# States of two directions summed on TensorE ahead of one product with C, and depthwise convolutions in 32-column tiles with their vertical taps on partitions

## The reference

```python
dA = jnp.exp(dt[:, :, None] * A)
h = dA * h + (dt * u_t)[:, :, None] * B_t[:, None, :]
y = jnp.einsum('bdn,bn->bd', h, C_t) + Dv * u_t
```

## Time and profile before

| | us |
|---|---|
| median of 3 executions | 24551.71 |
| lowest, highest | 24547.85, 24555.85 |
| span of the profiled execution, first to last instruction | 24540.0 |

### The profile page before, as it was taken

The page is one execution under the profiler, slowest core; times in us unless marked ns, Lnnn a source line. Parts: engine busy times, 40 slices in busy tenths (PEclk is TensorE's granted clock), DMA queues, the critical chain, the costliest instruction groups (busy, mean ns, idle before and its releaser), DMA issues. The chain is left out here.

```text
span 24540.0 us, 382078 instructions
## 1 busy us (share of the span) xinstructions
PE 20189.7 (82%) x128858; PEld 8709.5 (35%) x128858; DVE 22873.0 (93%) x21013; ACT 12682.8 (52%) x17667; POOL 8605.8 (35%) x4999
## 2 busy tenths in 40 slices
PE   5888888888888888888888888888888888888886
PEld 2333333333333333333333333333333333333332
DVE  5999999999999999999999999999999999999997
ACT  2555555555555555555555555555555555555554
POOL 2333333333333333333333333333333333333332
PEclk8888888888888888888888888888888888888886
DMA  2222222222222222222222222222222222222222
GB/s 72 75 77 66 78 76 68 78 71 72 77 66 78 76 67 78 72 71 78 68 76 76 67 78 75 68 78 69 74 79 66 78 74 69 78 70 73 77 67 64
DMA packets 646853, 1792.27 MB, mean 73 GB/s; under 512 B 76999, under 2 KB 87059, under 8 KB 644760
## 3 DMA queue, kind: packets, MB, share of 16 engines
q1 hardware_dynamic: 624280, 1726.94, 24.6%
q10 hardware_dynamic: 20480, 38.29, 0.5%
HBM read 1707.39 MB, written 44.96 MB: 71 GB/s over the span
## 5 line engine op out<-in xcount | busy, mean ns | idle before, releaser
L1502 POOL TENSOR_TENSOR drive<-du,Bb 128x784 f32<-128x784 f32 x3072 | 5678.1, 1848 | 14964.6 <-DVE drive L1135 14964.6
L461 PE MATMUL scan_sum<-prod,fold 64*64 64x392 f32 x40960 | 6186.6, 576 | 2824.0 <-DVE prod L1135 2821.4
L461 PE MATMUL bank<-pad,dg 64*64 64x392 f32 x61312 | 7421.5, 512 | 159.5 <-ACT pad L862 133.2
L862 ACT ACTIVATE decay_even<-delta,alog 128x784 f32<-128x784 f32 x3072 | 2818.1, 917 | 8475.7 <-DVE state L1292 8429.1
L1135 DVE TENSOR_TENSOR prod<-state,Cb 128x784 f32<-128x784 f32 x6144 | 6228.4, 1014 | 0.0
L1292 DVE TENSOR_TENSOR_SCAN state<-decay,drive 128x784 f32<-128x784 f32 x3072 | 5831.4, 1898 | 234.0 <-POOL drive L1502 16.0
L1292 DVE TENSOR_TENSOR_SCAN state<-decay_even,drive 128x784 f32<-128x784 f32 x3072 | 5500.0, 1790 | 336.9 <-ACT decay_even L862 172.1
L461 PEld LDWEIGHTS bank<-pad,dg 64*64 64x64 f32 x61312 | 3279.4, 142 | 3858.5 <-issue 3191.3
L461 PEld LDWEIGHTS scan_sum<-prod,fold 64*64 64x64 f32 x40960 | 1647.1, 146 | 6313.9 <-issue 4578.5
L1135 DVE TENSOR_TENSOR drive<-du,Bb 128x784 f32<-128x784 f32 x3072 | 2966.8, 966 | 55.1 <-issue 55.1
L862 ACT ACTIVATE decay<-delta,alog 128x784 f32<-128x784 f32 x3072 | 2862.7, 934 | 1.6
(11 more groups left out here) (179 smaller groups left out, 16842.7 us busy)
## 6 DMA issues: line engine op xcount, KB each, us to landing
Bb<-bc_rows SPq DMA_DIRECT2D x2048, 392.0 KB, 3.7
Cb<-bc_rows SPq DMA_DIRECT2D x2048, 392.0 KB, 4.2
xin<-in_x SPq DMA_DIRECT2D x64, 294.0 KB, 4.2
x_kept<-xin ACTq DMA_DIRECT2D x64, 294.0 KB, 4.4
x<-x_kept SPq DMA_DIRECT2D x64, 294.0 KB, 3.0
out_dram<-t SPq DMA_DIRECT2D x64, 294.0 KB, 2.6
crossed<-pwm ACTq DMA_DIRECT2D x128, 96.0 KB, 2.2
delta<-in_x SPq DMA_DIRECT2D x8, 1176.0 KB, 7.5
```

Source lines behind the costliest of these rows:

```text
L461: return pe.matmul(out, lhsT, rhs, start=start, stop=stop)
L862: return act.activation(out, in_, f, bias=bias, scale=scale, **more)
L1502: pool.tensor_tensor(drive[:, j % 2, :], du[:, m, :], Bb[:, q % SLOTS, :], ALU.mult).then_inc(drive_r.sem, 1)
```

## The change

The units are laid out anew: each has 64 channels on partitions 0 to 63 in one direction and the same channels on 64 to 127 in the other direction that runs the same way along L. Units come in 48 pairs, two states of the same channels and directions. There are still 96 scans, 96 decays and 96 drives. After a pair's second scan TensorE adds the two directions of both states with `fold` into a PSUM tile `S` (two states times 64 channels on partitions): four matmuls of 128x64 tiles. VectorE then does one product with C for the pair, read from `S`, and TensorE adds the two states into `Y` with two matmuls. The product of pair p-1 stands behind the first scan of pair p. Rings: `prod` 2 deep instead of 6, odd decays 2 instead of 3 and each asked for straight behind the even one, `state` 3. `S` takes two PSUM banks, so `Y` and `P` have one bank each; every use of `P` is a numbered round, filled by TensorE (`bank_filled`) and read by ScalarE or VectorE (`bank_read`), and each side waits for the other. B has a row per state for each third of the channels: 48 loads a sample; C has 24 pairs of half loads.

For the convolutions, the 576 channels go through `P` in nine chunks of 64; ScalarE's SiLU puts each chunk's padded image in SBUF, SP stores it to DRAM (2 DMAs a chunk) and loads it again five times, shifted by one row each, so that 24 channels times 5 vertical taps lie on 120 partitions (`rep`): 12 sets of 5 DMAs. One convolution tile is then 5 horizontal taps times 4 matmuls of 120x32, each with 32 output columns; there are 12 such tiles. The 3x3 one is alike: 3 stores of 2 DMAs, 3 sets of 6 loads, 36 matmuls of 96x32. Its result is copied to the other 64 partitions by DMA from ScalarE's queue (6 a sample). GpSimd fills the taps by 12 tensor_tensor instructions of 120x320 a sample in place of the diagonals. The expert stacks, `pww` and `dww`, no longer stay in SBUF and are loaded for each sample. A table gives the steps of the lead their slots: the 21 expansions and convolution tiles stand in 21 of the first 23 pairs, and ScalarE reads each one pair later; the tail is spread over units 15 to 94.5. The core of the diff:

```diff
-T0 = 5
-M0 = 9
+T0 = 6
+G = 4
+GC = C // G
+KT = 5
+KP = KT * GC
+TAPS = T0 * KT * G
+M0 = HID // 64
...
-KS = (0, 1, 3, 4, 2, 5)
-DECAYS = 3
-PRODS = 6
+DECAYS = 2
+PRODS = 2
+STATES = 3
+BSLOTS = 4
 SLOTS = 2
-UNITS = [(g, n, k) for g, ks in ((0, (0, 1, 3, 4)), (1, (2, 5))) for n in range(NS) for k in ks]
-NU = len(UNITS)
+PAIRS = [(s, m, r) for s in range(S3) for m in range(NS // 2) for r in range(2)]
+NP = len(PAIRS)
+NU = 2 * NP
+TURNS = NP // 2
+GROUP = NP // S3
...
-        Y = ps("scan_sum", 1024)
+        Y = ps("scan_sum", 512)
+        S = ps("state_sum", 1024)
         DP = ps("decay_even", 1024)
         TT = ps("pair", 1024)
-        PP = ps("bank", 1024)
+        P = ps("bank", 512)
         T = [TT[:, 0:512], TT[:, 512:1024]]
-        P = [PP[:, 0:512], PP[:, 512:1024]]
...
+            def shifted(i, span, h):
+                for t in range(T0):
+                    first, last = C * t // 64, (C * t + C - 1) // 64
+                    yield max(AT["expand", last] + READ + 2.0, AT["conv", t - 1, h] + 2.0 if t else 0.0)
+                    if t >= 1:
+                        sp.wait_ge(bank_filled.sem, bank(span, "conv", t - 1, h))
+                        alone()
+                    for c in range(first, last + 1):
+                        stored, count = image_out(c)
+                        sp.wait_ge(stored.sem, stored.at(i, count))
+                        alone()
+                    if t == 0 and not later(i):
+                        sp.wait_ge(s_border.sem, 16 * 2 * IMAGES)
+                    loaded, _ = rows_in(t, h)
+                    for dy in range(KT):
+                        src = hid_dram[C * t:C * t + C, PW * (14 * h + dy):PW * (14 * h + dy) + HROWS].rearrange("(g c) l -> c g l", g=G)
+                        sp.dma_start(rep[GC * dy:GC * dy + GC, h, :, :], src).then_inc(loaded.sem, 16)
...
+            def conv(i, span, t, h):
+                for dx, wait in enumerate((0.0, 0.3, 0.6, 1.2, 1.5)):
+                    yield AT["conv", t, h] + wait
+                    if dx == 0:
+                        pe.wait_ge(bank_read.sem, bank(span, "conv", t, h) - 1)
+                        loaded, count = rows_in(t, h)
+                        pe.wait_ge(loaded.sem, loaded.at(i, count))
+                        pe.wait_ge(taps_r.sem, taps_r.at(i, 2 * t + 2))
+                    for g in range(G):
+                        src = rep[0:KP, h, g, :].rearrange("p (y x) -> p y x", x=PW)[:, :, dx:dx + HW]
+                        last = mm(P[32 * g:32 * g + 32, 0:HALF], taps[:, t % 2, G * dx + g, :], src, start=dx == 0, stop=dx == KT - 1)
+                last.then_inc(bank_filled.sem, 1)
...
             def scan(i, *between):
-                for j, (g, n, k) in enumerate(UNITS):
-                    if j >= 1:
-                        summation(i, j - 1)
-                    go_on(between, j + 1)
+                for p in range(NP):
+                    if p >= 1:
+                        summation(i, p - 1)
+                    elif later(i):
+                        summation(i - 1, NP - 1)
+                    go_on(between, 2 * p + 1)
+                    pe.wait_ge(state_r.sem, state_r.at(i, 2 * p + 2))
+                    if p >= 1 or later(i):
+                        pe.wait_ge(prod_r.sem, prod_r.at(i, p))
+                    for h in range(2):
+                        for e in range(2):
+                            j = 2 * p + e
+                            last = mm(S[64 * e:64 * e + 64, 512 * h:512 * h + HALF], fold[:, :], half(state[:, j % STATES, :], h))
+                    last.then_inc(folded.sem, 1)
+                    go_on(between, 2 * p + 2)
                 go_on(between, END)
-                summation(i, NU - 1)
...
+            def summation(i, p):
+
+                s, m, r = PAIRS[p]
+                if p % GROUP == 0:
+                    if s >= 1 or later(i):
+                        pe.wait_ge(y_r.sem, y_r.at(i, s))
+                    pe.wait_ge(xc_in.sem, xc_in.at(i))
                     for h in range(2):
-                        last = mm(Y[64 * h:64 * h + 64, bank:bank + HALF], weights[rows], term[rows, h * HALF:(h + 1) * HALF],
-                                  start=start, stop=stop)
-                return last
-
-            def summation(i, j):
-
-                g, n, k = UNITS[j]
-                if n == 0 and k == (0, 2)[g]:
-                    skipped(i, g)
-                pe.wait_ge(prod_r.sem, prod_r.at(i, j + 1))
-                if g == 0:
-                    alone()
-                term = prod[:, j % PRODS, :] if k < 3 else prod[:, j % PRODS, ::-1]
-                spread(g, fold[:, :], term, False, n == NS - 1 and k == (4, 5)[g]).then_inc(summed.sem, 1)
+                        mm(Y[64 * h:64 * h + 64, 0:HALF], skip[:, s, :], half(xc[s], h), True, False)
+                pe.wait_ge(prod_r.sem, prod_r.at(i, p + 1))
+                term = prod[:, p % PRODS, :] if r == 0 else prod[:, p % PRODS, ::-1]
+                for h in range(2):
+                    last = mm(Y[64 * h:64 * h + 64, 0:HALF], fold[:, :], half(term, h), False, p % GROUP == GROUP - 1)
+                last.then_inc(summed.sem, 1)
...
                 for j in range(0, NU, 2):
                     decaying(j, DP[:, 0:L], 2, even_r)
-                    if j == 0:
-                        odd(1)
-                    if j + 3 < NU:
-                        odd(j + 3)
-                    if j == 66:
-                        act.wait_ge(summed.sem, summed.at(i, 64))
-                        ac(yk[:, :], Y[:, 512:512 + HALF], ACT.Copy).then_inc(yk_r.sem, 1)
+                    odd(j + 1)
...
-            def scan(i, ahead, *between):
-                def product(j):
-                    g, n, k = UNITS[j]
-                    q = turn(g, n)
-                    v.wait_ge(c_ld[q % SLOTS].sem, c_ld[q % SLOTS].at(i, 16 * (q // SLOTS + 1)))
-                    v.wait_ge(state_r.sem, state_r.at(i, j + 1))
-                    if j >= PRODS or later(i):
-                        v.wait_ge(summed.sem, summed.at(i, j - PRODS + 1))
-                    tt(prod[:, j % PRODS, :], state[:, j % 2, :], Cb[:, q % SLOTS, :], ALU.mult).then_inc(prod_r.sem, 1)
+                    tt(du[:, m, :], delta[:, m, :], u_of(m), ALU.mult).then_inc(du_r.sem, 1)
+
+            def scan(i, *between):
+                def product(i, p):
+                    q = p // 2
+                    v.wait_ge(c_ld[q % SLOTS].sem, c_ld[q % SLOTS].at(i, 32 * (q // SLOTS + 1)))
+                    v.wait_ge(folded.sem, folded.at(i, p + 1))
+                    if p >= PRODS or later(i):
+                        v.wait_ge(summed.sem, summed.at(i, p - PRODS + 1))
+                    tt(two(prod[:, p % PRODS, :]), banks(S), two(Cb[:, q % SLOTS, :]), ALU.mult).then_inc(prod_r.sem, 1)
 
                 def driving(j):
-                    g, n, k = UNITS[j]
-                    q = turn(g, n)
-                    v.wait_ge(b_ld[q % SLOTS].sem, b_ld[q % SLOTS].at(i, 16 * (q // SLOTS + 1)))
-                    m = KS.index(k)
-                    if n == 0:
-                        v.wait_ge(du_r.sem, du_r.at(i, m + 1))
+                    s, m, r = PAIRS[j // 2]
+                    b = 2 * (j // 4) + j % 2
+                    v.wait_ge(b_ld[b % BSLOTS].sem, b_ld[b % BSLOTS].at(i, 16 * (b // BSLOTS + 1)))
+                    if m == 0:
+                        v.wait_ge(du_r.sem, du_r.at(i, 2 * s + r + 1))
                     if j >= 2 or later(i):
                         v.wait_ge(state_r.sem, state_r.at(i, j - 1))
-                    if j == NU - 4 and ahead:
-                        v.wait_ge(bc_st.sem, bc_st.at(i + 1))
-                    tt(drive[:, j % 2, :], du[:, m, :], Bb[:, q % SLOTS, :], ALU.mult).then_inc(drive_r.sem, 1)
-
-                driving(0)
-                for j, (g, n, k) in enumerate(UNITS):
+                    tt(drive[:, j % 2, :], du[:, 2 * s + r, :], Bb[:, b % BSLOTS, :], ALU.mult).then_inc(drive_r.sem, 1)
+
+                def scanning(j):
                     if j % 2 == 0:
                         v.wait_ge(even_r.sem, even_r.at(i, j // 2 + 1))
                     else:
                         v.wait_ge(odd_r.sem, odd_r.at(i, j // 2 + 1))
                     v.wait_ge(drive_r.sem, drive_r.at(i, j + 1))
-                    if j >= 2 or later(i):
-                        v.wait_ge(prod_r.sem, prod_r.at(i, max(j - 1, 0)))
-                    v.tensor_tensor_scan(state[:, j % 2, :], DP[:, 0:L] if j % 2 == 0 else decay[:, j // 2 % DECAYS, :], drive[:, j % 2, :], 0.0,
+                    v.tensor_tensor_scan(state[:, j % STATES, :], DP[:, 0:L] if j % 2 == 0 else decay[:, j // 2 % DECAYS, :], drive[:, j % 2, :], 0.0,
                                          ALU.mult, ALU.add).then_inc(state_r.sem, 1)
-                    if j >= 1:
-                        product(j - 1)
-                    go_on(between, j)
-                    if j % 2 == 1 and j + 1 < NU:
```

(30 more changed lines are left out.)

971 lines of the change are left out of this document (472 added, 499 removed).

## The result

The changed kernel takes 24214.82 us (24196.8 to 24229.49, four runs), the kernel before beside it 24553.78: a ratio of 0.9862 [0.9848, 0.9876]. It is faster, by 339 us; forecast were 2170 us, and 24215 us lies outside the range of 21500 to 23500 us. The profiled execution has a span of 24195.0 us.

A forecast was written before the change was run, and what follows sets the result against it. It took VectorE to bound the kernel, TensorE next: 376.6 - 41.3 - 4.6 + (4 + 3 + 3 + 2) = 342.7 us a sample, 33.9 less. Over 64 samples that gave 22380 us, range 21500 to 23500.

The forecast's parts named there:

- VectorE's work: Scan loop: half the products go, 41.3 us a sample, and GpSimd's diagonals no longer slow scans and products, net 4.6 us.
- the slower rival: Convolutions: 32-column tiles don't run abreast, 2.88 us a step instead of 0.67, 28700 us in all; chance 0.08.
- Transfers: DMA loads of shifted rows and B and C rows: waits cost 2 us a sample (0 to 8).
- the rival with late rows: Convolutions: each of 12 sets of shifted rows comes 2.5 us late, 30 us a sample, 23530 us; chance 0.08.
- Change of shape: TensorE switching tile shapes: about 0.05 us a change, 10 us of its time, left inside the waits.
- Outside the loop: Set-up, first lead and last tail, 438 us of the span: change of 0 us (-40 to +60).
- VectorE's "99%": Support for the rival that VectorE still bounds (21610 to 23020 us, chance 0.64): its share of wall-to-wall time.
- TensorE, the waits: VectorE's product waiting for TensorE's sum: 4 us a sample in 12 pairs, 3 more for the low clock.
- the prediction's own sign of being wrong: VectorE's products waiting for TensorE's sums for over 20 us a sample.
- TensorE sets the pace: Rival: sums late in most pairs, waits of 27 us, period 358 us, 23360 us in all; chance 0.18.
- net -25 us: TensorE's busy time a sample: 160 us of new work against 185 gone, from 314 to some 289.
- -4.6 + 3 + 2: Terms a sample: GpSimd's diagonals gone (-4.6 us), ScalarE's table loads making decays late (3), transfers (2).

The follow-up runs named there:

- undone run: The changed kernel without the sum on TensorE, 96 products on VectorE again, a ring of three products and two state buffers: 25867 us, 1.0545 of the kernel before.
- g1: The changed kernel with TensorE's sums and summations made from a constant tile, without waits between it and VectorE's scans and products: 23404 us.
- h1: As g1, with ReLU in place of SiLU and the sigmoid, so no table loads in the loop: 22458 us.
- h4: The changed kernel with three of the five horizontal taps of each depthwise round left out: 23357 us.
- h5: The changed kernel with six unread matmuls of 120 columns added in each of 24 light pairs a sample: 24830 us.
- the late product: The changed kernel with each product behind the next pair's odd scan, four state and four B-row buffers: 23710 us, 0.9662 of the kernel before.

## Why the prediction was wrong

Right, point by point. **VectorE's work**: 48 products of 0.964 us (0.97 forecast), odd scans at 1.792 (1.79), 56 us a sample less instead of 46. Of the 56, products make 51 (96 x 1.014 - 48 x 0.964) and odd scans 5. Most of the ten more is counting: the forecast priced a product that goes at 0.86 us, from its start to the next start, while its busy time is 1.014, and 48 x 0.154 = 7.4. GpSimd's taps cost 63 odd scans some 0.5 us each, half a microsecond a sample (2.2 taken). **Tiles**: eight 32-column matmuls from 9750.19 to the next start at 9751.66, 0.735 us for four, so they run abreast (0.67 taken), and the slower rival is out. Five such steps make 3.7 us for a convolution tile, not 3.3. **Tables**: 53.6 loads a sample (54). **Transfers**: half a microsecond of waits for rows a sample (2 taken), so the rival with late rows is out. The rule beside it (the Trainium skill, "DMA: Bandwidth & Descriptors", the section on why a DMA increments its semaphore by 16) is neither borne out nor refuted: the profile gives no landing time for these loads. **Change of shape**: one depthwise step between other shapes takes 9748.58 to 9749.38, 0.80 us against 0.735, again about 0.06 us a change, as the row before had it. The drain that the Trainium skill names ("TensorEngine Tiling (Array Packing)", Key Properties) shows as no more than that. **Outside the loop**: 24195 - 64 x 372.0 = 387 us, 51 less than the 438 of before and just past the -40 allowed. VectorE's "99%" among the rivals holds for the second stretch of the earlier trace rows; over the ten samples of the earlier trace rows it is 95%.

The step that failed is "TensorE, the waits": "these 12 pairs are at the edge: 4 us a sample (0 to 12)", with 3 more for the low clock. Measured: 52, of which at most 496 / 64 = 8 are the sum's own length at the low clock and the rest its late start. This is the prediction's own sign of being wrong, products that wait for over 20 us a sample. It had given every pair the tail's average share, 1.2 us, and found 6.9 against 6.9. TensorE's work does not come in averages. It comes in blocks (two transforms 5.7 us, two pointwise rounds of six matmuls, two rounds of delta, B and C), some of them in pairs that hold a depthwise round already: 11.5 us against VectorE's 5.45. The low clock was read right in kind, and what holds TensorE there as well is ScalarE, whose results free the one bank. TensorE in order of time, after:

```profile
9674.63 1.67 PE L584 MATMUL bank<-dwo,wdl 6*128 6x392 f32 x2 [3.24 <-ACT du L914]
9676.23 2.88 PE L584 MATMUL state_sum<-state,fold 128*64 128x392 f32 x8
```

It waits 3.24 us for ScalarE, and the sum behind then takes 2.88 us (3.1 forecast). The nearest rival is "TensorE sets the pace", given 0.18 and 27 us: late sums in half of the pairs (1586 waits for 3072 products), at twice its size. That TensorE's pace is not the whole limit is what the experiments add.

Two things lay outside the working. First, "net -25 us" for TensorE was taken as relief. Measured are -14.6 us a sample (20189.7 and 19257.7 over 64). The undone run shows that everything but the sum, uneven and with a shorter ring, cost up to 20.5 us a sample, against next to nothing forecast for these parts (-4.6 + 3 + 2). Less the 25.8 of the sum this is the 5.3 gained (339 / 64), by construction, since both come from one run. Second, a wait that goes is not time that comes. Taking away 3326 us of it gave 817, since ScalarE (245 us of work a sample, and in order behind TensorE's rounds) was the next to be late. That the sum's wait hid these is shown by g1 and h1; that TensorE's load counts by some half where it was changed is shown by h4 and h5. No single resource was found that holds the 372 us: VectorE and TensorE have some 300 us each in a sample and ScalarE 245, all in strict orders that meet every few microseconds.

## What to carry to other kernels

When an operation moves onto another engine and back into the first one's circle, compare the two engines stretch by stretch between the hand-overs and add up the larger, not the sums of a whole period; where the engines' totals are within a few per cent of each other, blocks longer than the slack at the hand-over come back as waits (52 us a sample here, where averages gave 7). The sum of the larger loads is still a lower end: 349 of 378 us here, and setting TensorE free gave back only 811 us. Ask next what the wait hides: cut it in a run that leaves the rest alone, and price the change by that run. A hand-over one step later with one more buffer was worth more here (505 us) than moving blocks about (173), and both together 631.

## What the runs showed of the hardware

- TensorE's granted clock fell with its work, and the time rose all the same: 0.873 and 23807 us with the sums, 0.737 and 24004 us without. The clock rows of both:

```profile
core 0: 23805.3 us, clock 0.873
```

```profile
core 0: 24001.8 us, clock 0.737
```

- Six small matmuls in each of 24 light pairs raised it from 0.882 to 0.905, and the kernel lost 615 us.
- 32-column tiles with 120 rows run four abreast: 0.735 us for four matmuls of 392 columns in 32-bit floats, where one 128x128 matmul took 0.72.
- An odd scan of VectorE, which reads its decay and drive from SBUF, is slowed by a GpSimd instruction beside it: by the diagonals from 1.79 to 2.15 us, by a tap instruction of 0.72 us to 2.29 (the last two rows shown with the late product). An even scan, whose decay lies in PSUM, took 1.79 us with GpSimd's drive beside it almost from end to end (the same rows).
